# Fourier attention features: query units in pairs of 2048 elements, queries and keys scaled on ScalarE, four slots for the fractions

## The chip, the core and the metric

The kernel runs on one NeuronCore of a Trainium2 chip. PE is TensorE, ACT ScalarE, DVE VectorE, POOL GpSimd and SP SyncE; each runs its own stream of instructions strictly in the order written, and they meet through semaphores. The metric is the device time of one execution in microseconds (us). The kernel before was run three times: median 1554.88 us, from 1553.38 to 1557.7.

## The reference

The program is a two-layer decoder over 64 sequences of 64 tokens with 128 features (4096 tokens): self-attention, cross-attention, an expert layer, then a self-attention with Fourier features, a latent cross-attention and a quantised feed-forward layer. The change lies in the fourth step alone:

```python
def _fourier_kernel(x, proj_mat):
    p = jnp.einsum('blhd,dm->blhm', x, proj_mat) / math.sqrt(D_HEAD)
    return jnp.concatenate([jnp.cos(p), jnp.sin(p)], axis=-1) / math.sqrt(D_KMAP)
q = (x @ Wq.T + bq).reshape(Bv, Lv, N_HEAD, D_HEAD)
k = (x @ Wk.T + bk).reshape(Bv, Lv, N_HEAD, D_HEAD)
v = (x @ Wv.T + bv).reshape(Bv, Lv, N_HEAD, D_HEAD)
q_prime = _fourier_kernel(q, proj_mat)
k_prime = _fourier_kernel(k, proj_mat)
kv = jnp.einsum('blhm,blhd->bhmd', k_prime, v)
out = jnp.einsum('blhm,bhmd->blhd', q_prime, kv)
return out.reshape(Bv, Lv, D_MODEL) @ Wo.T + bo
```

There are 16 heads of 8 features, and 128 projections for each head, so every token has 2048 angles for its keys and 2048 for its queries; each needs a sine and a cosine.

## The kernel before

The Fourier stage works in 8 groups g of 512 tokens (four tiles of 128). A group has 16 units, numbered n; N counts them through all groups. A unit is 128 x 1024 angles: units 0 to 7 are the key half (two units for each tile of tokens, tokens on the partitions), units 8 to 15 the query half (two heads each, projections on the partitions, 512 tokens). The angles are held in turns, not radians.

The path of a unit:
- PE, `angles`: four matmuls into a pair of PSUM banks; there are two such pairs, so the angles of unit N wait until unit N - 2 is reduced. L895 for keys, L897 for queries.
- DVE, `reduce_`: `whole` is the angle rounded by adding and subtracting a large constant (L1258), `frac` the angle less that (L1266). For units 2, 5, 7, 10, 12 and 14 (`ON_SCALAR`) the first addition is made by ACT (`lift`, L1090, into `lifted`) and DVE does one instruction (L1263). Then `wrap` is the absolute value of `frac` (L1268). frac and wrap have three slots; a slot is free when the features of the unit three before are made.
- ACT, `features`: a sine of `frac` (L1082); behind it, where unit N + 2 is one of `ON_SCALAR`, the lift of that unit; then a cosine, which is a sine of a quarter turn less `wrap` (L1086). The results go to `feats` (keys) or `qf` (queries).
- PE, key half: `key_values` (L916) accumulates features times values; ACT copies the sum (`keep_kv`, L1096), PE turns it (L948), ACT copies it (`keep_turned`, L1114). There are two such halves for a group.
- PE, query half: for every two units `outputs` (L961), which ACT copies (`keep_o`, L1102); in the next group, behind its angles 4, `combine` (L975) multiplies with the output weights, and DVE adds the result to the stream (`residual`).
- Between these, the next group is prepared: PE transposes its tokens (L860), ACT copies them (`columns_of`, L1062), PE multiplies for keys (L867) and values (L869), DVE scales and shifts the keys (`keys`, L1234) and the values (L1242), then PE multiplies for the queries (L874) and DVE scales them (`queries`, L1249).

The order is written out by hand: each engine has one loop over N, and the conditions on n in it say what stands behind which unit. At n = 10 PE does the angles of unit 12, the outputs of units 8 and 9, and the transposes of the next group's tokens; the angles of unit 13 follow only then. The outputs wait for the cosine of unit 9 and for the second `keep_turned`.

Of the kernel before, what the change touches and what calls it, by code (L numbers as in the profile page):

```python
# [17 lines left out]
I32 = mybir.dt.int32  # L18
ALU = mybir.AluOpType
# [3 lines left out]
P = 128  # L23
# [686 lines left out]
def experts_and_fourier_phase(nc, ctx, c, name):  # L710
# [15 lines left out]
    KEYS = T * KU  # L726
    UPG = KEYS + Q4 * 2
    ALL = G * UPG
    RING = 3
    MAGIC = 1.5 * 2.0 ** 23  # L730
    TWO_PI, HALF_PI = 6.2831850, 1.5707962
    xs, xT = sb("xs", [P, T, P]), sb("xT", [P, T * P])
# [1 line left out]
    qT, kT = sb("qT", [P, T * P]), sb("kT", [P, T * P])  # L734
    projX = sb("projX", [P, H, M])
    vS = sb("vS", [P, 2, T // 2, H, 32])
    lifted = sb("lifted", [P, 2, UNIT])
    whole, frac, wrap = sb("whole", [P, UNIT]), sb("frac", [P, RING, UNIT]), sb("wrap", [P, RING, UNIT])
    feats = sb("feats", [P, RING, 8, 2, M])
    qf = sb("qf", [P, 2, 4, 2, T * P])  # L740
    kvs = sb("kvs", [P, Q4, 2, M])
# [51 lines left out]
    with nc.Block() as block:  # L793
# [237 lines left out]
        def _(act):  # L1031
# [32 lines left out]
            def features(N):  # L1064
                g, n = divmod(N, UPG)
                act.wait_ge(s["reduced"], N + 1)
                if n < KEYS:
                    used = g * KEYS + n - RING + 1 if n >= RING else g * KEYS
                    if used >= 1:
                        act.wait_ge(s["kv_ps"], used)  # L1070
                    sin, cos = feats[:, n % RING, :, 1, :], feats[:, n % RING, :, 0, :]
                    view = lambda a: a.rearrange("p (h m) -> p h m", m=M)
                else:
                    v = n - KEYS
                    if v % 2 == 0:
                        used = g * Q4 + v // 2 - 1
                        if used >= 1:
                            act.wait_ge(s["o_ps"], used)
                    h = (v % 2) * 2
                    sin, cos = qf[:, (v // 2) % 2, h:h + 2, 1, :], qf[:, (v // 2) % 2, h:h + 2, 0, :]  # L1080
                    view = lambda a: a.rearrange("p (h m) -> p h m", h=2)
                nc.scalar.activation(sin, view(frac[:, N % RING, :]), ACT.Sin, scale=-TWO_PI if n in ON_SCALAR else TWO_PI)  # L1082
                if N + 2 < ALL and (n + 2) % UPG in ON_SCALAR:
                    lift(N + 2)
                act.wait_ge(s["wrapped"], N + 1)
                nc.scalar.activation(cos, view(wrap[:, N % RING, :]), ACT.Sin, bias=half_pi[:, :], scale=-TWO_PI).then_inc(s["feats"], 1)  # L1086

            def lift(N):
                act.wait_ge(s["z_ps"], N + 1)
                nc.scalar.activation(lifted[:, lifts_before(N) % 2, :], angles_at(N), ACT.Copy, bias=MAGIC).then_inc(s["lifted"], 1)  # L1090

            def keep_kv(g, pair):
                act.wait_ge(s["kv_ps"], g * KEYS + 4 * pair + 4)
# [38 lines left out]
            for N in range(ALL + 5):  # L1132
                g, n = divmod(N, UPG)
                if g < G:
# [3 lines left out]
                        act.wait_ge(e["measured"], 2 * G)  # L1138
                    if N == KEYS - 2:
                        root(3, LATE)  # L1140
                    features(N)
                    if 3 <= N <= 6:
                        keep_products(N - 3)
                    if n == 4:
                        keep_kv(g, 0)
                    if g == 0 and n == 8:
# [8 lines left out]
                        keep_o(g, (n - KEYS - 3) // 2)  # L1155
                    if n == 10 and g + 1 < G:
                        columns_of(g + 1)
                if g == G and n == 0:
                    act.wait_ge(s["var"], 1)
                    nc.scalar.activation(c["rstd"][:, 0:MEASURED], c["rstd"][:, 0:MEASURED], ACT.Sqrt)  # L1160
                    nc.scalar.activation(rstdc[:, :], rstdc[:, :], ACT.Sqrt).then_inc(s["root"], 1)
# [8 lines left out]
        def _(dve):  # L1170
# [80 lines left out]
            def reduce_(N):  # L1251
                n = N % UPG
                z = angles_at(N)
                if n in ON_SCALAR:
                    dve.wait_ge(s["lifted"], lifts_before(N) + 1)
                else:
                    dve.wait_ge(s["z_ps"], N + 1)
                    nc.vector.tensor_scalar(whole[:, :], z, MAGIC, MAGIC, ALU.add, ALU.subtract).then_inc(s["rounded"], 1)  # L1258
                    dve.wait_ge(s["rounded"], N - lifts_before(N) + 1)
                if N >= RING:  # L1260
                    dve.wait_ge(s["feats"], N - RING + 1)
                if n in ON_SCALAR:
                    nc.vector.scalar_tensor_tensor(frac[:, N % RING, :], lifted[:, lifts_before(N) % 2, :], MAGIC, z,  # L1263
                                                   ALU.subtract, ALU.subtract).then_inc(s["reduced"], 1)
                else:
                    nc.vector.tensor_tensor(frac[:, N % RING, :], z, whole[:, :], ALU.subtract).then_inc(s["reduced"], 1)  # L1266
                dve.wait_ge(s["reduced"], N + 1)
                nc.vector.tensor_scalar(wrap[:, N % RING, :].bitcast(I32), frac[:, N % RING, :].bitcast(I32), 0x7FFFFFFF, None,  # L1268
                                        ALU.bitwise_and).then_inc(s["wrapped"], 1)

            def residual(g):
                x = c["stream"][:, g * T:(g + 1) * T, :]
# [81 lines left out]
            for N in range(ALL + 6):  # L1354
# [12 lines left out]
                if g < G:  # L1367
                    reduce_(N)
                    if g + 1 < G:
                        if n == KEYS + 5:  # L1370
                            keys(g + 1)
                            values(g + 1)
                if 1 <= g < G and n == 2:
                    queries(g)
                if g >= 1 and n == 4:
                    residual(g - 1)

# [1142 lines left out]
```

## Time and profile before

| what | value |
|---|---|
| median of three runs | 1554.88 us |
| profiled execution, its own time | 1560.69 us |
| its span, first to last instruction | 1558.9 us |
| PE busy over the span | 1414.6 us, 91% |
| DVE busy | 1120.7 us, 72% |
| ACT busy | 972.1 us, 62% |
| POOL busy | 297.5 us, 19% |
| mean granted TensorE clock | 0.976 |

The page cuts the span into 40 slices and gives each engine's busy share in tenths, one digit a slice. The Fourier stage lies in slices 14 to 23, where DVE shows mostly nines and ACT eights and nines:

```profile
PE   6999999998899788888988878999999999999984
PEld 4666666666566344343443355666666666666653
DVE  4666778886434899999999953455667776776788
ACT  2333367676554988998889943445655565665546
```

The shares over the whole span are means over six steps with different limits; what the changed step is limited by has to be read inside it.

### The profile page before, as it was taken

The numbers are of one execution on the slowest core, as the hardware profiler recorded it, in microseconds if no ns is written. First come the engines' busy times: TensorE is split into PE (matmuls) and PEld (weight loads), VectorE is DVE, ScalarE is ACT, GpSimd is POOL, SyncE is SP. The second block draws the span as 40 slices with busy tenths as digits, with TensorE's granted clock in tenths as the row PEclk, the third lists the DMA queues.
The fourth block names the chain that finished last, engine by engine and source line by source line (L and its number), as shares of the span: only waits on it lengthen the run. The fifth ranks groups of instructions, "written<-read, shape, count | busy, mean of one in ns | idle before, by whom it ended". The sixth has DMA issues, their size and how long they took to land. (4 is left out here: it accounts for less than half of the span.)

```text
span 1558.9 us, 32291 instructions
## 1 busy us (share of the span) xinstructions
PE 1414.6 (91%) x12651; PEld 869.2 (56%) x12666; DVE 1120.7 (72%) x2362; ACT 972.1 (62%) x1510; POOL 297.5 (19%) x274
## 2 busy tenths in 40 slices
PE   6999999998899788888988878999999999999984
PEld 4666666666566344343443355666666666666653
DVE  4666778886434899999999953455667776776788
ACT  2333367676554988998889943445655565665546
POOL 3433244452001011110110031111111112220000
PEclk9999999999899999999999989999999999999996
DMA  5000000000100000000000002222222222222210
GB/s 184 2 2 2 2 15 16 13 9 3 55 1 1 1 1 1 1 2 1 1 1 4 1 15 54 61 65 65 65 58 70 63 61 62 62 58 61 69 45 21
DMA packets 40246, 49.74 MB, mean 32 GB/s; under 512 B 8992, under 2 KB 22944, under 8 KB 39712
## 3 DMA queue, kind: packets, MB, share of 16 engines
q1 hardware_dynamic: 39808, 47.01, 11.8%
q8 instruction: 102, 1.67, 0.5%
q10 hardware_dynamic: 288, 0.67, 0.1%
q14 instruction: 48, 0.39, 0.1%
HBM read 13.04 MB, written 2.10 MB: 10 GB/s over the span
## 5 line engine op out<-in xcount | busy, mean ns | idle before, releaser
L2055 DVE TENSOR_TENSOR l_px<-psum,l_share 128x1024 f32<-128x1024 f32 x64 | 78.3, 1224 | 152.7 <-PE psum L1562 103.2
L1800 ACT ACTIVATE l_prob<-psum,l_bias 128x1024 f32<-128x1024 f32 x64 | 71.3, 1114 | 174.7 <-PE psum L1533 174.7
L1545 PE MATMUL psum<-l_XT,l_A 128*128 128x256 f32 x512 | 127.3, 394 | 1.5 <-ACT l_XT L1818 1.5
L1528 PE MATMUL psum<-l_th,l_XT 128*128 128x512 f32 x256 | 125.5, 613 | 1.4 <-DVE stream L2062 0.7
L1562 PE MATMUL psum<-l_prob,l_X 128*128 128x512 f32 x256 | 121.4, 596 | 0.7 <-DVE l_px L2055 0.7
L1608 PE MATMUL psum<-l_px,l_N 128*128 128x256 f32 x480 | 115.0, 383 | 0.0
L2032 DVE TENSOR_REDUCE l_top<-psum 128x8 bf16<-128x1024 f32 x64 | 78.1, 1220 | 36.5 <-PE psum L1625 36.5
L1545 PEld LDWEIGHTS psum<-l_XT,l_A 128*128 128x128 f32 x512 | 94.7, 195 | 12.7 <-ACT l_XT L1818 1.7
L1266 DVE TENSOR_TENSOR f_frac<-psum,f_whole 128x1024 f32<-128x1024 f32 x80 | 97.9, 1224 | 2.7
L1258 DVE TENSOR_SCALAR f_whole<-psum 128x1024 f32<-128x1024 f32 x80 | 97.3, 1217 | 1.6 <-PE psum L895 1.6
L1608 PEld LDWEIGHTS psum<-l_px,l_N 128*128 128x128 f32 x480 | 87.6, 190 | 16.1 <-issue 5.0
L1805 ACT COPY l_th<-psum 128x1024 f32<-128x1024 f32 x64 | 64.8, 1012 | 47.5 <-PE psum L1545 47.5
L408 ACT ACTIVATE a_probT<-psum 128x1024 f32<-128x1024 f32 x32 | 32.7, 1023 | 98.6 <-PE psum L199 98.6
L895 PE MATMUL psum<-f_projX,f_kT 64*128 64x512 f32 x256 | 74.0, 654 | 21.4 <-DVE f_frac L1266 10.6
L1268 DVE TENSOR_SCALAR f_wrap<-f_frac 128x1024 int32<-128x1024 int32 x128 | 88.8, 694 | 4.4
L669 POOL TENSOR_TENSOR a_KX<-a_KT,const 128x1024 f32<-128x1024 f32 x32 | 60.8, 1902 | 115.1 <-ACT a_KT L375 91.0
L480 DVE TENSOR_TENSOR a_prob<-psum,relbias 128x1024 f32<-128x1024 f32 x32 | 39.2, 1224 | 58.0 <-PE psum L185 52.5
L897 PE MATMUL psum<-f_qT,f_projX 64*128 64x512 f32 x256 | 72.1, 639 | 9.6 <-DVE f_frac L1266 9.5
L399 ACT ACTIVATE c_QX<-c_QT,const 128x128 f32<-128x128 f32 x256 | 78.5, 403 | 0.0
L916 PE MATMUL psum<-f_feats,f_vS 128*32 128x256 f32 x1024 | 69.4, 389 | 7.7 <-ACT f_feats L1086 3.7
L1082 ACT ACTIVATE f_feats<-f_frac 128x1024 f32<-128x1024 f32 x64 | 67.6, 1056 | 12.9 <-DVE f_frac L1266 12.9
L2355 POOL TENSOR_TENSOR l_hn<-l_hh,late_weights 128x1024 f32<-128x1024 f32 x12 | 28.2, 2349 | 246.6 <-DVE l_hh L2113 246.6
(353 smaller groups left out, 3193.4 us busy)
## 6 DMA issues: line engine op xcount, KB each, us to landing
l_share<-l_recip SPq DMA_DIRECT2D x496, 64.0 KB, 2.0
early_weights<-in_weights SPq DMA_DIRECT2D x1, 2405.0 KB, 11.4
c_cs<-in_ctx SPq DMA_DIRECT2D x16, 128.0 KB, 2.1
f_qf<-in_l_mats SPq DMA_DIRECT2D x1, 2048.0 KB, 7.7
out<-l_normed SPq DMA_DIRECT2D x16, 128.0 KB, 2.0
l_craw<-in_ctx SPq DMA_DIRECT2D x15, 128.0 KB, 2.3
late_weights<-in_weights SPq DMA_DIRECT2D x1, 1089.0 KB, 11.2
relbias<-in_relbias ACTq DMA_DIRECT2D x1, 512.0 KB, 5.2
```

What stands on the lines that cost most here:

```text
L399: last = nc.scalar.activation(QX[:, n % 3, :, j, :], QT[:, d % DUOS, t * P:(t + 1) * P].rearrange("p (b s) -> p b s", s=S), ACT.Copy, scal ...
L895: last = nc.tensor.matmul(out, kT[rows, t * P:(t + 1) * P], projX[rows, h:h + 4, :], start=True, stop=True)
L897: last = nc.tensor.matmul(out, projX[rows, n - KEYS + 8 * q, :], qT[rows, :], start=True, stop=True)
L1258: nc.vector.tensor_scalar(whole[:, :], z, MAGIC, MAGIC, ALU.add, ALU.subtract).then_inc(s["rounded"], 1)
L1266: nc.vector.tensor_tensor(frac[:, N % RING, :], z, whole[:, :], ALU.subtract).then_inc(s["reduced"], 1)
L1268: nc.vector.tensor_scalar(wrap[:, N % RING, :].bitcast(I32), frac[:, N % RING, :].bitcast(I32), 0x7FFFFFFF, None, ALU.bitwise_and).then_in ...
L1528: nc.tensor.matmul(ps[:, SC + n, :], XT[:, q % 3, k, :, :], th[:, q % 2, k, 8 * n:8 * n + 8, :], start=True, stop=False)
L1545: last = nc.tensor.matmul(ps[:, at + j // 2, (j % 2) * 256:(j % 2 + 1) * 256], A[:, QB * k + j, :], XT[:, q % 3, :, 1, :], start=True, sto ...
L1562: last = nc.tensor.matmul(ps[:, at + n, :], X[:, q % 2, k, :], prob[:, b % 4, n, :], start=True, stop=True)
L1608: last = nc.tensor.matmul(ps[:, YB, 0:256], N[:, h, :], px[:, q % 2, h, :, :], start=(h == 0), stop=(h == H - 1))
L2032: nc.vector.tensor_reduce(top[:, b % 4, :], ps[:, RO:RO + 2, :].rearrange("p a (j n) -> p (a j) n", n=P), AX.X, ALU.max, negate=True).then ...
L2055: nc.vector.tensor_tensor(px[:, q % 2, :, k, :], ps[:, at:at + 2, :].rearrange("p a (h s) -> p (a h) s", s=S), share[:, (b // 2) % 2, b % ...
```

## The change

The units of the query half are made into features two at a time. DVE still reduces each unit by itself, but takes the absolute value of both fractions of a pair in one instruction of 2048 elements behind the second; ACT does one sine and one cosine over 2048 elements for a pair. The lifts of units 10, 12 and 14 move on ACT: 10 stands alone at n = 8, 12 and 14 stand behind the pair (8, 9) and the pair (10, 11). `frac` and `wrap` have four slots in place of three. ACT writes its lift into the frac slot itself, in place of the tile `lifted`, and waits for that slot to be free. The sign of `frac` is now the same in all units. Scaling the queries and the keys of groups 1 to 7 moves from DVE to ACT; those of group 0 stay on DVE.

```diff
-    RING = 3
+    RING, FRACS = 3, 4
...
-    lifted = sb("lifted", [P, 2, UNIT])
-    whole, frac, wrap = sb("whole", [P, UNIT]), sb("frac", [P, RING, UNIT]), sb("wrap", [P, RING, UNIT])
+    whole, frac, wrap = sb("whole", [P, UNIT]), sb("frac", [P, FRACS, UNIT]), sb("wrap", [P, FRACS, UNIT])
...
+            def query_features(N):
+                g, n = divmod(N, UPG)
+                v = n - KEYS
+                at = N % FRACS
+                act.wait_ge(s["reduced"], N + 2)
+                used = g * Q4 + v // 2 - 1
+                if used >= 1:
+                    act.wait_ge(s["o_ps"], used)
+                sin, cos = qf[:, (v // 2) % 2, :, 1, :], qf[:, (v // 2) % 2, :, 0, :]
+                view = lambda a: a[:, at:at + 2, :].rearrange("p n (h m) -> p (n h) m", h=2)
+                nc.scalar.activation(sin, view(frac), ACT.Sin, scale=-TWO_PI)
+                act.wait_ge(s["wrapped"], N + 2)
+                nc.scalar.activation(cos, view(wrap), ACT.Sin, bias=half_pi[:, :], scale=-TWO_PI).then_inc(s["feats"], 2)
+                if n + 4 in ON_SCALAR:
+                    lift(N + 4)
...
             def lift(N):
                 act.wait_ge(s["z_ps"], N + 1)
-                nc.scalar.activation(lifted[:, lifts_before(N) % 2, :], angles_at(N), ACT.Copy, bias=MAGIC).then_inc(s["lifted"], 1)
+                if N >= FRACS:
+                    act.wait_ge(s["feats"], N - FRACS + 1)
+                nc.scalar.activation(frac[:, N % FRACS, :], angles_at(N), ACT.Copy, bias=MAGIC).then_inc(s["lifted"], 1)
+
+            def queries(g):
+                act.wait_ge(s["q_ps"], g + 1)
+                nc.scalar.activation(qT[:, :], ps[:, k_bank(g), :], ACT.Identity, bias=qb[:, :], scale=turn_scale).then_inc(s["q_sb"], 1)
+
+            def keys(g):
...
-                    features(N)
+                    if n < KEYS:
+                        features(N)
+                    elif n % 2 == 1:
+                        query_features(N - 1)
+                    elif n + 2 in ON_SCALAR and n == KEYS:
+                        lift(N + 2)
                     if 3 <= N <= 6:
                         keep_products(N - 3)
+                    if g >= 1 and n == 2:
+                        queries(g)
...
+                    if n == 12 and g + 1 < G:
+                        keys(g + 1)
...
+                units = 2 if n >= KEYS else 1
                 dve.wait_ge(s["reduced"], N + 1)
+                if units == 2 and n % 2 == 0:
+                    return
+                at = (N + 1 - units) % FRACS
+                if N >= FRACS:
+                    dve.wait_ge(s["feats"], N - FRACS + 1)
+                nc.vector.tensor_scalar(wrap[:, at:at + units, :].bitcast(I32), frac[:, at:at + units, :].bitcast(I32), 0x7FFFFFFF, None,
+                                        ALU.bitwise_and).then_inc(s["wrapped"], units)
...
                         if n == KEYS + 5:
-                            keys(g + 1)
                             values(g + 1)
-                if 1 <= g < G and n == 2:
-                    queries(g)
```

The order on ACT in the query half, from the first `keep_turned` (L1114, later L1130) of a group that has a next group. f_frac -> f_qf is a query sine, f_wrap -> f_qf a cosine, f_lifted or f_frac from psum a lift, f_kvs `keep_kv`, f_xT the copy of the next tokens. Before:

```order
L1114 COPY f_kvm<-psum 128x1024
L1082 ACTIVATE f_qf<-f_frac 128x2x512
L1090 ACTIVATE f_lifted<-psum 128x1024
L1086 ACTIVATE f_qf<-f_wrap,f_half_pi 128x2x512
L1096 COPY f_kvs<-psum 128x1024
L1082 ACTIVATE f_qf<-f_frac 128x2x512
L1086 ACTIVATE f_qf<-f_wrap,f_half_pi 128x2x512
L1114 COPY f_kvm<-psum 128x1024
L1082 ACTIVATE f_qf<-f_frac 128x2x512
L1090 ACTIVATE f_lifted<-psum 128x1024
L1086 ACTIVATE f_qf<-f_wrap,f_half_pi 128x2x512
L1062 COPY f_xT<-psum 128x512
```

After:

```order
L1130 COPY f_kvm<-psum 128x1024
L1098 ACTIVATE f_frac<-psum 128x1024
L1112 COPY f_kvs<-psum 128x1024
L1088 ACTIVATE f_qf<-f_frac 128x4x512
L1090 ACTIVATE f_qf<-f_wrap,f_half_pi 128x4x512
L1098 ACTIVATE f_frac<-psum 128x1024
L1130 COPY f_kvm<-psum 128x1024
L1061 COPY f_xT<-psum 128x512
L1088 ACTIVATE f_qf<-f_frac 128x4x512
L1090 ACTIVATE f_qf<-f_wrap,f_half_pi 128x4x512
L1098 ACTIVATE f_frac<-psum 128x1024
L1118 COPY f_oT<-psum 128x512
```

Between the first `keep_turned` and the copy of f_xT stand units 8, 9 and 10 with their lifts of 10 and 12 before, and only units 8 and 9 with the same two lifts after; unit 10 is now part of a double sine and cosine behind the copy.

The order on DVE in the same half, from the reduction of unit 12 (its lifted form, f_frac from a lifted angle) through that of unit 15; f_whole and f_frac reduce, f_wrap is the absolute value, f_kT the keys, f_vS the values. Before:

```order
L1263 SCALAR_TENSOR_TENSOR f_frac<-f_lifted,psum 128x1024
L1268 TENSOR_SCALAR f_wrap<-f_frac 128x1024
L1258 TENSOR_SCALAR f_whole<-psum 128x1024
L1266 TENSOR_TENSOR f_frac<-psum,f_whole 128x1024
L1268 TENSOR_SCALAR f_wrap<-f_frac 128x1024
L1234 TENSOR_SCALAR f_kT<-psum,f_kb 128x512
L1242 SCALAR_TENSOR_TENSOR f_vS<-psum,f_vb 64x32x8 x4
L1263 SCALAR_TENSOR_TENSOR f_frac<-f_lifted,psum 128x1024
L1268 TENSOR_SCALAR f_wrap<-f_frac 128x1024
L1258 TENSOR_SCALAR f_whole<-psum 128x1024
L1266 TENSOR_TENSOR f_frac<-psum,f_whole 128x1024
L1268 TENSOR_SCALAR f_wrap<-f_frac 128x1024
```

After:

```order
L1282 SCALAR_TENSOR_TENSOR f_frac<-f_frac,psum 128x1024
L1285 TENSOR_SCALAR f_whole<-psum 128x1024
L1289 TENSOR_TENSOR f_frac<-f_whole,psum 128x1024
L1297 TENSOR_SCALAR f_wrap<-f_frac 128x2048
L1267 SCALAR_TENSOR_TENSOR f_vS<-psum,f_vb 64x32x8 x4
L1282 SCALAR_TENSOR_TENSOR f_frac<-f_frac,psum 128x1024
L1285 TENSOR_SCALAR f_whole<-psum 128x1024
L1289 TENSOR_TENSOR f_frac<-f_whole,psum 128x1024
L1297 TENSOR_SCALAR f_wrap<-f_frac 128x2048
```

Four absolute values of 1024 became two of 2048, each behind the second unit of its pair, and the keys are gone from before the values.

## Rows read from the trace of the kernel before

**Rows 1.** Busy times by window, of one group's period; first the view's columns.

```profile
core 0: us, PE busy (x) PEld busy (x) DVE busy (x) ACT busy (x) POOL busy (x), PEclk, DMA share, GB/s
...
560.54:608.83 48.29, 42.46 (x418) 19.41 (x416) 46.37 (x59) 43.89 (x48) 5.28 (x5) 1.00 0.01 2
```

**Rows 2.** Groups of instructions of DVE, 505 to 900 us: the absolute value.

```profile
L1268 DVE TENSOR_SCALAR f_wrap<-f_frac 128x1024 int32<-128x1024 int32 x128 | 88.8, 694 | 4.4
```

**Rows 3.** Timeline of group 1, query half: start, duration, engine, line, operation.

```profile
587.11 1.13 PE L897 MATMUL psum<-f_qT,f_projX 64*128 64x512 f32 x4
...
588.17 1.07 PE L916 MATMUL psum<-f_feats,f_vS 128*32 128x256 f32 x16
...
590.63 1.02 ACT L1096 COPY f_kvs<-psum 128x1024 f32<-128x1024 f32 x1
591.52 1.08 ACT L1082 ACTIVATE f_qf<-f_frac 128x1024 f32<-128x1024 f32 x1
...
592.48 1.16 ACT L1086 ACTIVATE f_qf<-f_wrap,f_half_pi 128x1024 f32<-128x1024 f32 x1
...
593.52 1.02 ACT L1114 COPY f_kvm<-psum 128x1024 f32<-128x1024 f32 x1
...
594.68 1.93 PE L961 MATMUL psum<-f_qf,f_kvm 128*32 128x256 f32 x32 [0.83 <-ACT f_kvm L1114]
...
595.37 1.04 ACT L1090 ACTIVATE f_lifted<-psum 128x1024 f32<-128x1024 f32 x1
...
596.44 1.22 DVE L1263 SCALAR_TENSOR_TENSOR f_frac<-f_lifted,psum 128x1024 f32<-128x1024 f32 x1 [0.89 <-ACT f_lifted L1090]
...
597.13 1.13 PE L897 MATMUL psum<-f_qT,f_projX 64*128 64x512 f32 x4
597.31 0.61 ACT L1062 COPY f_xT<-psum 128x512 f32<-128x512 f32 x1
...
598.31 1.22 DVE L1258 TENSOR_SCALAR f_whole<-psum 128x1024 f32<-128x1024 f32 x1
...
601.44 0.75 DVE L1234 TENSOR_SCALAR f_kT<-psum,f_kb 128x512 f32<-128x512 f32 x1
602.10 1.72 DVE L1242 SCALAR_TENSOR_TENSOR f_vS<-psum,f_vb 64x256 f32<-64x256 f32 x4
...
608.83 1.22 DVE L1258 TENSOR_SCALAR f_whole<-psum 128x1024 f32<-128x1024 f32 x1
```

**Rows 4.** Timeline: the key half of group 1, and one row of group 2.

```profile
568.63 0.75 DVE L1249 TENSOR_SCALAR f_qT<-psum,f_qb 128x512 f32<-128x512 f32 x1
...
570.30 3.71 PE L975 MATMUL psum<-early_weights,f_oT 128*64 128x128 f32 x64
...
575.12 1.03 ACT L1090 ACTIVATE f_lifted<-psum 128x1024 f32<-128x1024 f32 x1 [2.27 <-PE psum L895]
...
614.47 1.13 PE L895 MATMUL psum<-f_projX,f_kT 64*128 64x512 f32 x4
```

**Rows 5.** Groups of instructions of ACT, 505 to 900 us: cosine, sine, lift.

```profile
L1086 ACT ACTIVATE f_qf<-f_wrap,f_half_pi 128x1024 f32<-128x1024 f32 x64 | 74.0, 1156 | 0.0
...
L1082 ACT ACTIVATE f_qf<-f_frac 128x1024 f32<-128x1024 f32 x64 | 69.0, 1078 | 2.7 <-DVE f_frac L1266 2.7
...
L1090 ACT ACTIVATE f_lifted<-psum 128x1024 f32<-128x1024 f32 x48 | 49.3, 1026 | 18.8 <-PE psum L895 17.9
```

**Rows 6.** Groups of instructions of ACT, whole span: shorter forms.

```profile
L1054 ACT ACTIVATE f_qf<-f_qf 128x512 f32<-128x512 f32 x32 | 20.2, 630 | 1.0
...
L1844 ACT ACTIVATE l_r<-psum,l_deq 128x512 f32<-128x512 f32 x26 | 16.2, 672 | 0.5 <-DMA c_cs<-in_ctx 0.5
```

**Rows 7.** Timeline of group 0, query half.

```profile
539.70 1.09 PE L948 MATMUL psum<-const,f_kvs 128*128 128x128 f32 x8
...
545.22 1.03 ACT L1114 COPY f_kvm<-psum 128x1024 f32<-128x1024 f32 x1
```

**Rows 8.** Timeline of the last group: the last cosine.

```profile
897.83 1.18 ACT L1086 ACTIVATE f_qf<-f_wrap,f_half_pi 128x1024 f32<-128x1024 f32 x1
```

More of the change, by code:

```diff
@@ L1072, in features @@
                     view = lambda a: a.rearrange("p (h m) -> p h m", m=M)
[L1073 to L1082, printed above, removed]
+                nc.scalar.activation(sin, view(frac[:, N % FRACS, :]), ACT.Sin, scale=-TWO_PI)
                 if N + 2 < ALL and (n + 2) % UPG in ON_SCALAR:
@@ L1085, in features @@
                 act.wait_ge(s["wrapped"], N + 1)
-                nc.scalar.activation(cos, view(wrap[:, N % RING, :]), ACT.Sin, bias=half_pi[:, :], scale=-TWO_PI).then_inc(s["feats"], 1)
+                nc.scalar.activation(cos, view(wrap[:, N % FRACS, :]), ACT.Sin, bias=half_pi[:, :], scale=-TWO_PI).then_inc(s["feats"], 1)
+            def query_features(N):
[13 more added lines that the diff above has]
+                    lift(N + 4)
             def lift(N):
                 act.wait_ge(s["z_ps"], N + 1)
-                nc.scalar.activation(lifted[:, lifts_before(N) % 2, :], angles_at(N), ACT.Copy, bias=MAGIC).then_inc(s["lifted"], 1)
+                if N >= FRACS:
[5 more added lines that the diff above has]
+            def keys(g):
+                act.wait_ge(s["k_ps"], g + 1)
+                nc.scalar.activation(kT[:, :], ps[:, k_bank(g), :], ACT.Identity, bias=kb[:, :], scale=turn_scale).then_inc(s["k_sb"], 1)
             def keep_kv(g, pair):
@@ L1253, in reduce_ @@
                 z = angles_at(N)
+                part = frac[:, N % FRACS, :]
                 if n in ON_SCALAR:
                     dve.wait_ge(s["lifted"], lifts_before(N) + 1)
+                    nc.vector.scalar_tensor_tensor(part, part, MAGIC, z, ALU.subtract, ALU.subtract).then_inc(s["reduced"], 1)
                 else:
@@ L1259, in reduce_ @@
                     dve.wait_ge(s["rounded"], N - lifts_before(N) + 1)
[L1260 to L1266, printed above, removed]
-                dve.wait_ge(s["reduced"], N + 1)
-                nc.vector.tensor_scalar(wrap[:, N % RING, :].bitcast(I32), frac[:, N % RING, :].bitcast(I32), 0x7FFFFFFF, None,
-                                        ALU.bitwise_and).then_inc(s["wrapped"], 1)
+                    if N >= FRACS:
+                        dve.wait_ge(s["feats"], N - FRACS + 1)
+                    nc.vector.tensor_tensor(part, whole[:, :], z, ALU.subtract).then_inc(s["reduced"], 1)
+                units = 2 if n >= KEYS else 1
+                dve.wait_ge(s["reduced"], N + 1)
+                if units == 2 and n % 2 == 0:
+                    return
+                at = (N + 1 - units) % FRACS
+                if N >= FRACS:
+                    dve.wait_ge(s["feats"], N - FRACS + 1)
+                nc.vector.tensor_scalar(wrap[:, at:at + units, :].bitcast(I32), frac[:, at:at + units, :].bitcast(I32), 0x7FFFFFFF, None,
+                                        ALU.bitwise_and).then_inc(s["wrapped"], units)
             def residual(g):
```

## The prediction

> **What bounds the kernel now.** I first read the busy times by window, to see how full the engines are where the change works. Eight groups of 16 units run from 504 to 897 us. Six of them, from group 1 on, have the same period of 48.29 us, in which DVE is busy 46.37 us, ACT 43.89 and PE 42.46, at a granted TensorE clock of 1.00 [rows 1]. So the first suspicion is DVE at 96%, and the absolute values are 128 instructions of 694 ns there [rows 2]. The timeline must say whether DVE is truly never kept waiting. In the query half of group 1 it waits once, 0.89 us, for the lift of unit 12, and its next unit (13, at 598.31) starts the moment that the angles of unit 13 end on PE (597.13 + 1.13 = 598.26) [rows 3]. These angles stand on PE behind a chain through ACT: keep_kv 590.63, keep_turned 593.52, outputs 594.68, transposes of the next tokens, angles 13. ACT works without a gap from keep_kv to its copy of xT at 597.31. Two engines are thus equally late at that place: DVE has about a microsecond to spare there, and ACT's order of work sets when PE may go on. In the key half PE's combine (3.71 us from 570.30) holds back the angles of unit 5, for which ACT waits 2.27 us before its lift at 575.12 [rows 4].
>
> **The change part by part.** Start-to-start times decide on a full queue. For ACT I read them in rows 3: sine to cosine 0.96, cosine to the next 1.04 (its 1.16 less an overlap of 0.12), a 1024 copy 0.89; and for a lift 0.91 (its 1.03 less the same overlap).
>
> *One sine and one cosine over 2048.* The trace has no such instruction. From below: a 1078 ns sine [rows 5] against a 630 ns SBUF form of 512 elements [rows 6] gives 448 ns for 512, or 0.83 to 0.90 for 1024 more; from above: 1.08 and 1.16, as if nothing were saved. I take 0.85, so a double sine occupies ACT 1.81 us and a double cosine 1.89. A pair costs 3.70 in place of 4.00 in four instructions, 1.2 us less of ACT per group. The Trainium skill ("ScalarE: Activation LUTs", What ACT_TABLE_LOAD costs) gives 186 ns + 0.833 ns an element, 280 with a bias pointer, and 93 ns of overlap. The single forms in rows 5 agree within 4%, and by it the double forms would occupy 1.80 and 1.89.
>
> *One absolute value over 2048.* Bounds: the cost of one, 0.69, and of two, 1.39. A single one holds DVE 0.61, since the next starts at the overlap of 0.08; I take 1.15 for the double, between 0.7 and 1.22. That is 0.3 us less of DVE per group (four pairs of 1.22 against 1.15), between nothing and 2.1.
>
> *Keys and queries on ACT.* DVE loses 0.66 twice (601.44 to 602.10 in rows 3; the same form at 568.63 in rows 4). ACT gains two scaled copies of 512 from PSUM with a pointer, whose like takes 672 ns [rows 6], 0.57 start to start. Below, a plain 512 copy's 0.46; above, 0.67. Behind the queries at n = 2 stand sine 3 and the lift of unit 5, which waits 2.27 us for PE: hidden. Behind the keys stand the sine and cosine of units 12 and 13.
>
> *Four slots.* DVE's only wait in rows 3 is the lift's, none is for a slot, so the fourth slot gives nothing but the room that pairs need. The lift into the frac slot adds a wait: the lift of unit 12 now stands behind ACT's own double cosine and waits until it has ended, 0.12 + 0.04 us.
>
> *The order on ACT.* This is what costs. Before, ACT reaches keep_turned at 593.52 after sine 8, lift 10, cosine 8, keep_kv, sine 9, cosine 9. And between keep_turned and the copy of xT it has three instructions of unit 10 to do while PE works. Now, on ACT: keep_turned, lift 10, keep_kv, double sine, double cosine, lift 12, keep_turned, copy of xT, all ahead of the next double sine. Laid out for group 1 from the rows:
> - angles 10 on PE end at 588.24 and key_values 7 at 588.17 + 1.07 = 589.24, as before. The key features ahead of them don't change. The lift of unit 10 starts at 588.28, keep_kv at 589.28.
> - Double sine 590.17, double cosine 591.98; its end, 593.98, releases the lift of unit 12 at 594.02.
> - keep_turned 594.93, in place of 593.52: 1.41 later. Outputs, transposes, angles 13, xT and DVE's unit 13 all follow it with the distances of rows 3: outputs 596.09, angles 13 at 598.54, xT at 598.72, DVE's unit 13 at 599.72 in place of 598.31. ACT meanwhile stands idle from 595.82 to 598.72. DVE would be ready for unit 13 at 598.31 - 0.89 (the lift is there in time now) - 0.75 (two double absolute values in place of five single ones) = 596.67, and waits 3.05 us for PE.
> - From 598.31 to the next group's first unit at 608.83 DVE takes 10.52 us. It loses 0.66 for the keys. It does two double absolute values where three single ones stood (two of 1.15 for three of 0.61): +0.47. That is 10.33; the next group starts at 610.05, 1.22 late. I looked at what could be later still: the lift of unit 14 (after the double cosine that starts at 601.00) ends at 604.06, wanted by DVE at about 605.1; the angles of unit 15, behind the outputs that wait for the same cosine, end at 606.12, wanted at 606.36. Both fit.
> - The last double cosine of the group ends at 612.95. Behind it PE does outputs and then angles 3 of the next group, at 615.83, where 614.47 [rows 4] plus 1.22 would be 615.69: 0.14 more. From there key_values, combine, angles 5 and lift 5 follow back to back on PE and ACT as in rows 4. The 0.66 of the queries that DVE no longer has ends at this gate: DVE only meets the lift of unit 7 a few tenths early, and what it gains by that ACT can't use, for it works from lift 5 through cosine 7 without a gap.
>
> So a full group costs 1.22 + 0.14 = 1.36 us more, and there are six: 8.2. In group 0 the turn of the first key-value half on PE (539.70 + 1.09) gates keep_turned at 540.83; keep_kv 541.72, double sine 542.61, double cosine 544.42, lift 12 546.46, keep_turned 547.37 against 545.22 [rows 7]: +2.15, less 0.19, plus 0.14 = 2.1. The last group has no next tokens, but its last features come in one piece: the same layout from its rows ends the last cosine at 900.12 in place of 897.83 + 1.18 = 899.01 [rows 8]: 1.1. Sum: 8.2 + 2.1 + 1.1 = 11.4 us. Against the profiled execution's own 1560.69 us that is 1572.1; the median of the three runs is 1554.88, to which I add the same: 1566.3.
>
> The Trainium skill ("VectorE: DVE Perf Modes", The TRN2 errata) says that a fixed latency is paid between instructions, so that large tiles pay it once, and that one should tile larger. That rule speaks for this change; what it would yield is the first rival.
>
> **Rivals.**
> *DVE bounds and the waits move.* If ACT's order had slack at the copy of xT, each full group would win on DVE the keys and queries 1.32, the absolute values 0.28 and the 0.89 wait: 2.5 us. Six groups 15, less in the first and last: about 14 us, 1541. The 96% of rows 1 speak for it. Against it: the distance from keep_turned to DVE's unit 13 in rows 3 is all PE and ACT, with no gap that could absorb 1.4 us. It decides if PE could do angles 13 before the transposes, which its order forbids.
>
> *Partly given back.* If DVE's 0.66 at the queries did carry through the key half, a full group would cost 1.36 - 0.66 = 0.7, and all 4.2 + 3.2 = 7.4: 1562. If the double forms also lay at 0.83 and the double absolute value near 0.7, a pair would be 0.04 shorter and the tail after unit 13 0.9 shorter: 0.7 - 0.9 - 0.1 = -0.3 a group, -1.8 for six, against 3.2 for the first and last: 1.4 in all, 1556.
>
> *Double forms that save nothing.* At 1.08 and 1.16 more, keep_turned comes 0.54 later, and the second pair's end another 0.54 later, which then passes the 0.24 of room at unit 15: 0.8 to 1.1 a group, 7 to 9 us more: 1574.
>
> **How the numbers follow.** Forecast 65%, its own range 1562 to 1570; double forms that save nothing 8%; partly given back 14%, of which half lies within 0.3%; DVE bounds 10%; 3% for what I don't see. The range from 1551 to 1574 reaches over the second and third rival and leaves out DVE's. 0.3% (4.7 us) is about what a measurement of this kernel tells from no change. Faster 0.11, same 0.09, slower 0.80.
>
> **What would show it.** In the changed profile: a period of 49.6 us for groups 1 to 6; an idle time of ACT of about 2.9 us before each copy of xT in them, ended by PE's transposes; DVE waiting about 3 us for the angles before unit 13, and no longer for the lift of unit 12; the double sine near 1.93 and the double cosine near 2.01 us; ACT's wait before lift 5 shorter than 2.27 but there. DVE's busy time falls by about 1.3 per group although the time rises. I am wrong if the period is below 48.3 or if ACT's idle time before xT is under 1 us.

## The result, and the profile after

The changed kernel takes 1586.24 us (median of five runs, 1583.97 to 1587.9), the kernel before 1553.38 in its five (1551.07 to 1557.7): a ratio of 1.0199, 95% interval 1.018 to 1.0219. It is slower, as forecast, but by 2.0% and not by the 0.7% that I forecast: 1566.3 was 20 us too low, and 1586 lies outside my range, which ended at 1574.

The profiled execution took 1587.9 us with a span of 1586.1. A group now takes 52.0 to 52.7 us (from one residual's statistics on DVE to the next, mean 52.39 over five groups; the sixth takes 51.2) against 48.29 [rows 1], where I forecast 49.65. The stage, from DVE's first rounding to the aggregation of the last residual's statistics, takes 433.45 us in place of 405.87: 27.6 more, about the difference of the profiled spans, 27.2. The medians differ by 32.9, 5.3 more than the stage: the profiled execution of the kernel before took 1560.69 us, 7 above its median, that of the changed kernel only 2 above. The work ahead of the stage ends anywhere between 499 and 506 us in the profiles below, so I leave these few microseconds open and compare the stage.

The timeline of the changed kernel, query half of group 1, corresponds to rows 3. L1098 is the lift, L1112 `keep_kv`, L1088 and L1090 the double sine and cosine, L1130 `keep_turned`, L960 the outputs, L859 the transposes, L1061 the copy of xT, L1285 DVE's rounding (of unit 13 at 605.28, of the next group's unit 0 at 616.03), L1297 the absolute value:

```profile
591.10 1.02 ACT L1098 ACTIVATE f_frac<-psum 128x1024 f32<-128x1024 f32 x1 [0.44 <-PE psum L896]
...
592.12 1.01 ACT L1112 COPY f_kvs<-psum 128x1024 f32<-128x1024 f32 x1
...
593.03 1.92 ACT L1088 ACTIVATE f_qf<-f_frac 128x2048 f32<-128x2048 f32 x1
...
594.21 1.13 PE L896 MATMUL psum<-f_qT,f_projX 64*128 64x512 f32 x4
594.85 1.99 ACT L1090 ACTIVATE f_qf<-f_wrap,f_half_pi 128x2048 f32<-128x2048 f32 x1
...
596.93 1.02 ACT L1098 ACTIVATE f_frac<-psum 128x1024 f32<-128x1024 f32 x1
597.85 1.00 ACT L1130 COPY f_kvm<-psum 128x1024 f32<-128x1024 f32 x1
...
599.00 3.64 PE L960 MATMUL psum<-f_qf,f_kvm 128*32 128x256 f32 x32 [3.66 <-ACT f_kvm L1130]
...
602.57 1.12 PE L859 MATMUL psum<-const,f_xs 128*128 128x128 f32 x4
...
603.73 0.59 ACT L1061 COPY f_xT<-psum 128x512 f32<-128x512 f32 x1 [4.87 <-PE psum L859]
...
605.28 1.23 DVE L1285 TENSOR_SCALAR f_whole<-psum 128x1024 f32<-128x1024 f32 x1 [6.07 <-PE psum L896]
...
607.85 1.53 DVE L1297 TENSOR_SCALAR f_wrap<-f_frac 128x2048 int32<-128x2048 int32 x1
...
616.03 1.22 DVE L1285 TENSOR_SCALAR f_whole<-psum 128x1024 f32<-128x1024 f32 x1
```

Up to `keep_turned` it is the layout to 0.1 us: from the lift of unit 10 to it 6.75, laid out as 6.65. What isn't in the layout is the next row. PE is idle for 3.66 us before the outputs, and the outputs then take 3.64 where they took 1.93, the transposes 1.12 where they took 0.66. From `keep_turned` to DVE's unit 13 it is 7.43 us; in rows 3 it was 4.79. The windows of the same kernel give the clock of just this stretch, as PEclk:

```profile
core 0: us, PE busy (x) PEld busy (x) DVE busy (x) ACT busy (x) POOL busy (x), PEclk, DMA share, GB/s
...
599.00:605.28 6.28, 6.28 (x41) 2.97 (x42) 0.21 (x1) 1.55 (x2) 1.48 (x2) 0.56 0.01 3
```

Granted is 0.56 of full speed, nearly all of it at the lower of TensorE's two levels, 1.2 GHz in place of 2.4. The outputs take 1.71 us more than before, the transposes 0.46, the angles of unit 13 0.41 (1.54 for 1.13): 2.58 of the 2.64 that are added between `keep_turned` and unit 13. The waits of PE show the gap in all eight groups, and the outputs behind it take 2.92 to 3.64 us in all eight:

```profile
PE psum L960 <- ACT f_kvm L1130: 29.3, 8, 3.7
```

The double forms cost what was worked out (estimates were 1.93 and 2.01 us). The groups of instructions of ACT, then of DVE:

```profile
L1090 ACT ACTIVATE f_qf<-f_wrap,f_half_pi 128x2048 f32<-128x2048 f32 x32 | 63.9, 1996 | 0.0
L1088 ACT ACTIVATE f_qf<-f_frac 128x2048 f32<-128x2048 f32 x32 | 61.3, 1917 | 3.4 <-DVE f_frac L1289 3.4
```

```profile
L1297 DVE TENSOR_SCALAR f_wrap<-f_frac 128x2048 int32<-128x2048 int32 x32 | 42.5, 1329 | 2.9
```

The double absolute value is 1.23 us where nothing disturbs it and up to 1.96 where POOL works at the same time, 1.33 in the mean.

### The profile page after: what moved, and what is told of

Read it like the earlier page. It is cut to its first block and busy times, and to the rows that moved or that the text cites. A ratio compares the mean times of both kernels' runs of the same rounds, so it can differ in the third digit from the quotient of the medians.

```text
span 1586.1 us, 32364 instructions
## 1 busy us (share of the span) xinstructions
PE 1427.5 (90%) x12666; PEld 873.5 (55%) x12666; DVE 1114.2 (70%) x2316; ACT 973.6 (61%) x1460; POOL 292.4 (18%) x274
## 5 line engine op out<-in xcount | busy, mean ns | idle before, releaser
L1285 DVE TENSOR_SCALAR f_whole<-psum 128x1024 f32<-128x1024 f32 x80 | 97.6, 1220 | 45.1 <-PE psum L896 42.5
L960 PE MATMUL psum<-f_qf,f_kvm 128*32 128x256 f32 x1024 | 75.6, 445 | 40.1 <-ACT f_kvm L1130 29.3
L1289 DVE TENSOR_TENSOR f_frac<-f_whole,psum 128x1024 f32<-128x1024 f32 x80 | 97.7, 1221 | 2.7
L1297 DVE TENSOR_SCALAR f_wrap<-f_frac 128x1024 int32<-128x1024 int32 (+1 forms) x96 | 86.9, 905 | 5.1
L960 PEld LDWEIGHTS psum<-f_qf,f_kvm 128*32 128x32 f32 x1024 | 35.8, 124 | 87.2 <-issue 51.4
L1417 POOL TENSOR_SCALAR f_xs<-stream,moments,rstd 128x128 f32<-128x128 f32 x28 | 21.9, 796 | 293.0 <-PE psum L859 292.8
```

What stands on the lines that cost most here:

```text
L960: last = nc.tensor.matmul(ps[32 * r:32 * r + 32, 4 + q % 2, toks], kvm[:, pair, q, e, 32 * r:32 * r + 32], qf[:, q % 2, r, e, toks], start ...
L1289: nc.vector.tensor_tensor(part, whole[:, :], z, ALU.subtract).then_inc(s["reduced"], 1)
L1297: nc.vector.tensor_scalar(wrap[:, at:at + units, :].bitcast(I32), frac[:, at:at + units, :].bitcast(I32), 0x7FFFFFFF, None, ALU.bitwise_an ...
```

## The experiments

Every kernel is compared with the kernel before on the same chip; ratios have 95% intervals. "Period" is the distance of the residuals' statistics on DVE between full groups; "stage" is as in the section above, from each run's profile.

| run | median us | ratio to before | period us | stage us |
|---|---|---|---|---|
| before | 1553.38 | 1 | 48.3 | 405.9 |
| after | 1586.24 | 1.0199 (1.018 to 1.0219) | 52.0 to 52.7 | 433.5 |
| e1_fill | 1577.49 | 1.0128 (1.0098 to 1.0159) | 50.5, then 51.1 | 423.4 |
| e2_kq_back | 1584.52 | 1.0168 (1.0135 to 1.02) | 51.2 | 428.3 |
| e3_kq_only | 1552.53 | 0.9968 (0.9951 to 0.9985) | 47.65 | 398.4 |
| e4_turned_early | 1548.74 | 0.9955 (0.9937 to 0.9972) | 47.2 to 48.3 | 402.3 |
| e5_lift_early | 1547.65 | 0.9962 (0.9949 to 0.9976) | 47.4 | 399.4 |
| e6_delay_only | 1591.43 | 1.0245 (1.0228 to 1.0262) | 52.2 to 53.8 | 438.0 |
| e7_single_abs | 1573.48 | 1.0132 (1.0115 to 1.015) | 50.3 | 419.5 |
| e8_four_forms | 1592.99 | 1.0254 (1.0239 to 1.0269) | 52.1 to 54.1 | 442.4 |
| e9_single_best | 1545.59 | 0.9933 (0.9912 to 0.9954) | 47.0 | 394.1 |

The kernel before took 1557.63 us in the comparison with e1 to e4, 1554.19 in that with e5 to e8, and 1556.77 in that with e9. So the medians of two rows can differ by a few microseconds for that alone; ratios and stages compare better.

**PE kept busy in the gap.** Only this is added to the changed kernel's PE:

```diff
+                    if n == KEYS + 2:
+                        for _ in range(3):
+                            nc.tensor.matmul(ps[:, 5, :], w("f_wk"), w("f_wo")[:, 0:512], start=True, stop=True)
                     if n >= KEYS + 2 and n % 2 == 0:
                         outputs(g, n // 2 - 5)
```

> The changed kernel with three added matmuls of 128x512 on PE in every group, between the angles of unit 12 and the outputs of units 8 and 9, where PE stands idle for 3.66 us; their result is thrown away. Theory (the idle time costs PE its clock): the outputs fall from 3.1 to 3.6 us back to 1.93, the transposes from 1.12 to 0.66, the granted clock of that stretch from 0.56 to about 1.0; DVE's unit 13 comes 4.8 us behind the start of keep_turned in place of 7.4; 2.6 us less in each of seven groups and about 1.4 in the last: 1566 us (1563 to 1570). Rival (the outputs are slow for what they read or write, the double forms on ACT and DVE): outputs stay above 3 us, and the time at 1586.

More work on PE makes the kernel 9 us faster by the medians and the stage 10 us shorter; 1566 was expected (1563 to 1570), so this is a good part of it and not all. Its timeline in group 1 (L1016 the three added matmuls, which the profile counts as six, L1133 `keep_turned`, L1288 DVE's unit 13, L1424 POOL's addition, L1300 the absolute value):

```profile
592.10 2.84 PE L1016 MATMUL psum<-early_weights 128*128 128x512 f32 x6
...
594.68 1.01 ACT L1133 COPY f_kvm<-psum 128x1024 f32<-128x1024 f32 x1
...
595.83 1.93 PE L960 MATMUL psum<-f_qf,f_kvm 128*32 128x256 f32 x32 [0.89 <-ACT f_kvm L1133]
...
599.53 1.23 DVE L1288 TENSOR_SCALAR f_whole<-psum 128x1024 f32<-128x1024 f32 x1 [3.49 <-PE psum L896]
...
601.67 1.29 POOL L1424 TENSOR_TENSOR stream<-f_xs,early_weights 128x512 f32<-128x512 f32 x1
602.10 1.95 DVE L1300 TENSOR_SCALAR f_wrap<-f_frac 128x2048 int32<-128x2048 int32 x1
```

`keep_turned` to unit 13 is 4.85 in all seven groups with a next one, close to the 4.79 of rows 3, and the outputs behind the gap take 1.93; the granted clock from 595.83 to 599.50 is 1.00. So the clock is the cause of that part. What is missing: group 1 takes 50.5, later groups 51.1. In groups 2 to 5 the outputs of units 12 and 13 run at the lower level instead (3.3 to 3.6 us). And the absolute value of units 12 and 13 falls under POOL's addition and takes 1.95 in group 1, where it took 1.53 in the changed kernel (in groups 2 and 3 it took 1.94 and 1.96 there too).

**The delay without the pairs.** The kernel before, one copy moved:

```diff
-                    if n == 9:
+                    if n == 10:
                         keep_turned(g, 1)
```

> The kernel before with one thing moved: ACT does the second keep_turned behind the features of unit 10 and not behind those of unit 9. Nothing is paired. Theory (a late keep_turned costs its delay and, by PE's idle time, the clock): keep_turned 2.9 us later, PE idle 3.7 us in place of 0.83, the outputs at 3.1 to 3.6 us and a granted clock near 0.56 behind it, period 53.8, 1594 us (1588 to 1600). Rival (delay alone, the clock in the changed kernel falls for its double forms): period 51.2, outputs 1.93, 1575.

```profile
597.28 1.03 ACT L1114 COPY f_kvm<-psum 128x1024 f32<-128x1024 f32 x1
...
598.46 3.34 PE L961 MATMUL psum<-f_qf,f_kvm 128*32 128x256 f32 x32 [3.73 <-ACT f_kvm L1114]
...
602.42 0.58 ACT L1062 COPY f_xT<-psum 128x512 f32<-128x512 f32 x1 [4.11 <-PE psum L860]
...
705.83 1.94 PE L961 MATMUL psum<-f_qf,f_kvm 128*32 128x256 f32 x32 [3.73 <-ACT f_kvm L1114]
```

This kernel has neither double forms nor a changed engine for anything, and shows the same: 3.73 us of PE idle, outputs of 3.34, 1591 us. So the double size isn't needed for the fall of the clock. The third row, of group 3, shows that the gap doesn't always bring it: behind the same 3.73 us the outputs take 1.94 there and 1.93 in the last group, and 2.44 to 3.34 in the other six. That parts the price. Group 3 takes 52.2 us, 3.9 more than before, without a fall of the clock: most of it is 2.9 for the delay itself and 0.8 because the absolute value of unit 13 now comes behind POOL's addition and takes 1.53 in place of 0.70, which neither theory had. Groups 2 and 4 take 53.8; the 1.6 more are the clock.

**The pair in four instructions.**

```diff
-                nc.scalar.activation(sin, view(frac), ACT.Sin, scale=-TWO_PI)
+                for i in range(2):
+                    nc.scalar.activation(qf[:, (v // 2) % 2, 2 * i:2 * i + 2, 1, :], view(frac, i), ACT.Sin, scale=-TWO_PI)
                 act.wait_ge(s["wrapped"], N + 2)
```

(and the cosine likewise)

> The changed kernel with the pair's sine and cosine in four instructions of 1024 elements in the same place on ACT: sine, sine, cosine, cosine; the features are signalled behind the last. Theory (the place costs, the size gains 0.3 us a pair): keep_turned 0.3 us later, PE idle 3.9 us, 0.3 to 0.9 us a group: 1591 us (1588 to 1594). Rival (the double size itself costs): 1580 or less.

```profile
599.09 3.19 PE L960 MATMUL psum<-f_qf,f_kvm 128*32 128x256 f32 x32 [3.94 <-ACT f_kvm L1132]
```

The total is as expected, and the rival is refuted: with single forms in the same place the kernel is no faster, but 6.8 us slower (1592.99 against 1586.24; the stage 8.9). `keep_turned` comes 8.47 us behind the first one in place of 8.19, and PE's gap is 3.94. The place on ACT is what costs. The 6.8 us are not all saved by the double forms themselves, though. In groups 2, 3 and 5, with periods of 54.0 to 54.1, the outputs of units 12 and 13 run at the lower level as well (3.23 to 3.62 us); in the changed kernel that happens in group 5 alone (3.46). In groups 1 and 4, where it doesn't, the period is 52.1 and 52.2, no longer than the changed kernel's 52.7.

**Single absolute values**, with the three added matmuls kept:

```diff
-                units = 2 if n >= KEYS else 1
+                units = 1
```

> As the run with three added matmuls, but the absolute value over 1024 elements for each unit, behind its own reduction; double sine and cosine kept. Theory (behind unit 13 DVE works without a gap, and a double absolute value there stands for one of two that would have been hidden in the wait, and is held up beside POOL's additions): from unit 13 to the next group 10.0 us in place of 11.2, seven groups: 1569 us (1566 to 1572). Rival (fewer, larger instructions are what saves): 0.3 us a group slower, 1579.

A miss: 1573.5 us, above the 1566 to 1572 expected. The period is 50.28 in each of five groups, and all outputs in them take 1.93; the stage is 3.9 us shorter than with the double values. The ratios of the two runs, 1.0128 and 1.0132, don't tell them apart; only the profiles do, and part of the difference there is the clock. Group 1 compares the two without it, since all its outputs take 1.93 in both: from unit 13 to the next group 10.69 us with single values and 11.17 with double ones, 0.48 less and not the 1.2 of the theory, because even the single value of unit 13 stands under POOL's addition; over the whole group 0.23 less (50.28 against 50.51). So the price of the double value is shown in its place, and it is small; it isn't shown in the total.

```profile
601.37 1.29 POOL L1424 TENSOR_TENSOR stream<-f_xs,early_weights 128x512 f32<-128x512 f32 x1
601.68 1.53 DVE L1300 TENSOR_SCALAR f_wrap<-f_frac 128x1024 int32<-128x1024 int32 x1
```

**Queries and keys back on DVE**

```diff
+                            keys(g + 1)
                             values(g + 1)
+                if 1 <= g < G and n == 2:
+                    queries(g)
```

(and taken out of ACT's loop)

> The changed kernel with the scaling of queries and keys back on DVE, pairs and four slots kept. Theory (the second part of the query half, behind unit 13, runs on DVE without a gap, the key half is gated by PE and ACT): the keys cost 0.66 in each of seven groups, the queries nothing: 1591 us (1589 to 1593). Rival (ACT's load is what the change made too large): ACT wins 1.2 us a group, seven groups: 1578.

A miss: 1584.5, not 1591. The work did cost DVE its 0.66 behind unit 13 (11.80 us from there to the next group, where groups 2 and 3 of the changed kernel take 11.16 and 11.17), but behind this gap the clock didn't fall in the six full groups; the last row is of the last group:

```profile
600.30 1.01 ACT L1130 COPY f_kvm<-psum 128x1024 f32<-128x1024 f32 x1
...
601.46 1.93 PE L960 MATMUL psum<-f_qf,f_kvm 128*32 128x256 f32 x32 [3.31 <-ACT f_kvm L1130]
...
907.81 3.64 PE L960 MATMUL psum<-f_qf,f_kvm 128*32 128x256 f32 x32 [3.32 <-ACT f_kvm L1130]
```

PE's angles of unit 12 wait 0.28 us for DVE here and end 2.15 us ahead of `keep_turned`, not 2.51, so the gap is 3.31 us in place of 3.66. In group 0, which has no queries in its loop, the gap is 3.66 and the outputs take 3.21. But the shorter gap is not the whole reason: in the last group it is 3.32, and the outputs take 3.64.

**Queries and keys alone on ACT**, in the kernel before (the changed kernel's functions, at n = 2 and n = 12).

> The kernel before with only the scaling of queries and keys moved to ACT (queries behind the features of unit 2, keys at n = 12); single features, three slots. Theory: keys win 0.66 in each of seven groups, the queries nothing, since the gate at unit 5 stands on PE: 1549 us (1547 to 1552). Rival (DVE bounds the whole stage): 1.3 a group, 1544. Second rival (ACT is as full as DVE, its cosine of unit 13 comes late): no gain, 1553.

The median, 1552.5 us, is just above the range given; it is 5 us below the kernel before in the same comparison, which is what the theory took off. The period is 48.29 less 0.65: the keys' 0.66 comes through (9.86 us from unit 13 to the next group in place of 10.52), the queries' doesn't (26.3 us from the group's first rounding to the first `keep_turned` in both). DVE gives 0.41 of it back in a longer wait for the lift of unit 12, 1.30 where rows 3 have 0.89:

```profile
590.46 1.22 DVE L1275 SCALAR_TENSOR_TENSOR f_frac<-f_lifted,psum 128x1024 f32<-128x1024 f32 x1 [1.30 <-ACT f_lifted L1090]
```

**Another order for the pairs**

```diff
                 nc.scalar.activation(sin, view(frac), ACT.Sin, scale=-TWO_PI)
+                if n == KEYS:
+                    keep_turned(g, 1)
                 act.wait_ge(s["wrapped"], N + 2)
...
-                    if n == 9:
-                        keep_turned(g, 1)
...
-                    if n >= KEYS + 2 and n % 2 == 0:
+                    if n >= KEYS + 3 and n % 2 == 0:
                         outputs(g, n // 2 - 5)
+                    if n == KEYS + 3:
+                        outputs(g, 0)
```

> The changed kernel with another order at one place: ACT does the second keep_turned between the double sine and the double cosine of units 8 and 9, and PE does the transposes of the next tokens and the angles of unit 13 ahead of the outputs of units 8 and 9. Theory (what costs is that all of ACT's pair stands ahead of keep_turned, and PE idle behind it): PE's idle time before the transposes about 0.6 us, its clock 1.0, DVE's unit 13 about 5.2 us earlier in a group, limited now by the lift of unit 12; period 47.2 in place of 52.4: 1547 us (1543 to 1553), below the kernel before. Rival (pairs of 2048 are late for their users wherever the copies stand): above 1565.

37 us faster than the changed kernel by the medians, and 31 in the stage, with the same instructions; two orders changed, that of one copy on ACT and that of the outputs on PE, and the run doesn't part them. L1134 is `keep_turned`, L859 the transposes, L1284 DVE's unit 12:

```profile
588.62 1.00 ACT L1134 COPY f_kvm<-psum 128x1024 f32<-128x1024 f32 x1
...
589.77 0.63 PE L859 MATMUL psum<-const,f_xs 128*128 128x128 f32 x4 [0.65 <-ACT f_kvm L1134]
...
592.68 1.22 DVE L1284 SCALAR_TENSOR_TENSOR f_frac<-f_frac,psum 128x1024 f32<-128x1024 f32 x1 [0.98 <-ACT f_frac L1102]
```

Groups 3 and 5 are 1 us longer; there the clock falls later, behind two gaps of 0.90 and 0.84 us, which the other groups have too without it:

```profile
697.20 3.62 PE L960 MATMUL psum<-f_qf,f_kvm 128*32 128x256 f32 x32 [0.84 <-ACT f_qf L1094]
```

**The lift ahead of the cosine, and a little work for PE at n = 14** (in the kernel of e4; `filler` is one matmul of 256 columns whose product is overwritten, added to PE on each side of the angles)

```diff
+                    act.wait_ge(s["sined"], g + 1)
+                    lift(N + 4)
...
+                if g < G and n == KEYS + 6:
+                    filler(g)
                 if N + 2 < ALL:
                     angles(N + 2)
+                if g < G and n == KEYS + 6:
+                    filler(g)
```

> As the run with the early keep_turned, and besides: the lift of unit 12 also ahead of the double cosine of units 8 and 9 (it waits for the double sine and the absolute value alone, which are the readers of its slot), and two matmuls of 128x256 on PE at n = 14, around the angles of the next group's unit 0, their result thrown away. Theory: DVE's wait of 0.98 before unit 12 goes, of which 0.6 to 0.9 reaches the next group; the outputs of units 12 and 13, which ran at half the clock (3.6 us) in every second group, take 1.93 in all: period 46.6, stage about 8 us shorter than the kernel before's, 1543 us (1539 to 1548). Rival (ACT, which works without a gap from unit 10's sine into the next group, is the bound now): no faster than the early keep_turned alone, 1549.

The outputs take 1.93 in all full groups and the period is even, 47.4; but what the wait of 0.98 gave is lost again. The absolute value of units 12 and 13 now meets POOL's addition and takes 1.72 us, where it took 1.23 in e4_turned_early, and DVE waits another 0.44 for PE before unit 15:

```profile
592.09 1.29 POOL L1434 TENSOR_TENSOR stream<-f_xs,early_weights 128x512 f32<-128x512 f32 x1
...
592.74 1.72 DVE L1310 TENSOR_SCALAR f_wrap<-f_frac 128x2048 int32<-128x2048 int32 x1
```

The total, 1547.65, lies inside the range of the theory and at the value of the rival, and its interval overlaps that of e4_turned_early. No gain is shown over it; that ACT is the bound is not shown either.

**The better version, without pairs**

```diff
+                if n + 2 == KEYS + 4:
+                    lift(N + 2)
                 nc.scalar.activation(sin, view(frac[:, N % RING, :]), ACT.Sin, scale=-TWO_PI if n in ON_SCALAR else TWO_PI)
```

(with e3_kq_only's move and PE's order as in e4_turned_early)

> The kernel before with queries and keys scaled on ACT, single features and three slots, and two changes of order: ACT lifts unit 12 ahead of the sine of unit 10, and PE does the transposes and the angles of unit 13 ahead of the outputs of units 8 and 9. Theory: DVE's wait of 1.30 us before unit 12, which keys and queries on ACT alone leave, falls to about 0.3, nothing else comes late: period 46.8 in place of 47.65, 1543 us (1540 to 1548), faster than all before it. Rival (PE's keys and values, which still follow the outputs, or ACT, which has hardly a gap left, hold the group at the old pace): 47.6, 1549.

```profile
588.58 0.63 PE L860 MATMUL psum<-const,f_xs 128*128 128x128 f32 x4 [0.83 <-ACT f_kvm L1126]
...
589.40 1.22 DVE L1279 SCALAR_TENSOR_TENSOR f_frac<-f_lifted,psum 128x1024 f32<-128x1024 f32 x1 [0.36 <-ACT f_lifted L1094]
```

0.9933 of the kernel before, 11 us, and 2.6% below the changed kernel by the ratio of the ratios. PE's gap is 0.83, DVE's wait before unit 12 0.36 in place of 1.30. It is the fastest in these runs; its interval still overlaps those of e4 and e5.

## Why the prediction was right in direction and wrong in size

The later `keep_turned` came as predicted and set the direction; what it did to PE was missing from the sum. For the first full group (group 1, 52.67 us, 4.38 more than before), and for the six from group 1 on together:

| step | forecast, group 1 | measured, group 1 | forecast, six | measured, six |
|---|---|---|---|---|
| `keep_turned` later | 1.41 | 1.51 | 8.5 | 9.0 |
| `keep_turned` to DVE's unit 13 | 0 | 2.64 | 0 | 11.7 |
| unit 13 to the next group | -0.19 | +0.23 | -1.1 | +2.1 |
| next group's start to its first `keep_turned` (angles 3 late) | 0.14 | 0 | 0.8 | 0.6 |
| sum | 1.36 | 4.38 | 8.2 | 23.4 |

Group 1 is one of the two dearest: the second step added 2.6 and 2.7 us in groups 1 and 4, and 1.4 to 1.7 in the others, with the clock's fall longer or shorter.

**The step that failed** is "Outputs, transposes, angles 13, xT and DVE's unit 13 all follow it with the distances of rows 3". Those distances were taken at full clock behind a gap of 0.83 us. I had worked out that ACT would stand idle for 2.9 us and DVE for 3.05, but never laid out PE, the engine they both waited for. It had finished the angles of unit 12 at 595.34 and had nothing until 599.00. e1_fill takes the 2.64 away with the gap; in e6_delay_only a later copy alone makes such a loss appear, in six groups of eight. The six periods from group 1 on sum to 313.2 us where they were 289.8: 23.4 more, of which the forecast had 8.2. Of the 15.2 that it lacks, 11.7 lie in this step. The whole stage lacks 27.6 - 11.4 = 16.2.

The trace of before had the price in it. Three rows of its timeline, early key angles of the stage and its last two outputs, none of them among my rows:

```profile
511.80 2.08 PE L895 MATMUL psum<-f_projX,f_kT 64*128 64x512 f32 x4 [3.41 <-DVE f_frac L1266]
...
894.61 1.93 PE L961 MATMUL psum<-f_qf,f_kvm 128*32 128x256 f32 x32 [2.37 <-ACT f_qf L1086]
...
899.06 2.88 PE L961 MATMUL psum<-f_qf,f_kvm 128*32 128x256 f32 x32 [2.51 <-ACT f_qf L1086]
```

2.08 us stands there for what takes 1.13 elsewhere, and 2.88 for 1.93. The row between them kept its 1.93 behind a gap of 2.37 us, so these rows give the price of a fall and a warning, but not when it comes. The Trainium skill ("TensorE: Matmul & The Clock Gate", Why this matters for your kernels) warns of idle gaps between bursts of matmuls for this very reason. In the changed kernel the trace agrees, in all eight groups; in e6_delay_only six of eight do. I weighed two other pages instead of this one.

**The tail behind unit 13** was mis-sized by 0.4 in group 1: a double absolute value of 1.45 start to start for 1.15 beside POOL, and 0.06 more between a fraction and a double value, twice. In groups 2 and 3, where the double value takes 1.94 and 1.96, it was mis-sized by 0.8 (11.16 and 11.17 us in place of 10.33). Working out +0.47 for "two of 1.15 for three of 0.61" was right in sign: one of two values is moved out of a stretch in which DVE waits anyway into one in which it doesn't.

**Right:** the double sine and cosine (1.92 and 2.00 us against 1.93 and 2.01); the lift behind its own cosine; the gap of ACT before xT, 4.87 us, of which 2.9 was forecast and the rest is the clock; that the queries give nothing and the keys 0.66 (e3_kq_only); DVE's wait before unit 13, 6.07 where I had 3.05 plus, again, the clock. The ends: up to the statistics of group 1 the stage took 2.4 us more, where I had 2.1 for group 0, and the last group cost about 1.7 by its interval (44.83 against 43.08), where I had 1.1.

**The rivals:** "DVE bounds" is refuted, DVE's busy time fell (1120.7 to 1114.2 us over the span) and the time rose. "Partly given back" is refuted too: the queries' 0.66 doesn't carry through (e3_kq_only), and the double absolute value takes 1.23 alone, not 0.7. "Double forms that save nothing" is refuted by the rows, 1.92 and 2.00 us for two of 1.08 and 1.16. None of my cases had an upper end above 1574, because all of them kept PE's speed.

What stays open: the 5.3 us between the difference of the medians and that of the stages, and what decides whether the clock falls. It fell behind 3.73 us in six groups of e6_delay_only and not in two, behind gaps of under 1 us in some groups of e4_turned_early and e1_fill and not in others.

## What to carry to other kernels

When a change delays a producer, lay out the idle time of every engine behind it, PE first, and look in the trace for what the same matmuls took behind such a gap: a few microseconds of idle PE were charged twice here, once as the gap and once at half the clock. Fusing two instructions saves their fixed cost (0.3 us a pair here), but everything queued behind them waits for both; put copies that others wait for between the parts. Here the place of one copy on ACT, with PE's order to suit, was worth 31 us of the stage, and fusing sine and cosine 9 at most, part of which was the clock. The best kernel found has no pairs at all.

## What the runs showed of the hardware

- In the changed kernel a gap of 3.66 us of PE was followed by outputs of 2.92 to 3.64 us in place of 1.93 in all eight groups, in group 1 at a granted clock of 0.56. The length of one gap alone doesn't tell, though. Behind 3.73 us in e6_delay_only six groups show 2.44 to 3.34 us and two 1.93 and 1.94; behind 3.31 to 3.35 us in e2_kq_back six groups show 1.93 and the last 3.64; behind two gaps of 0.90 and 0.84 us in a row in e4_turned_early two groups show 3.61 and 3.62 and the others 1.93.
- A DVE absolute value issued at 602.10 while POOL's addition ran from 601.67 to 602.96 (e1_fill) ended at 604.05: 1.95 us in place of 1.23, 1.09 behind POOL's end. The single one at 601.68 in e7_single_abs took 1.53 in place of 0.69. In the kernel before DVE's was issued first and kept its 0.70, and POOL's addition took 1.74 in place of 1.29:

```profile
600.83 0.70 DVE L1268 TENSOR_SCALAR f_wrap<-f_frac 128x1024 int32<-128x1024 int32 x1
600.94 1.74 POOL L1395 TENSOR_TENSOR stream<-f_xs,early_weights 128x512 f32<-128x512 f32 x1
```

  The Trainium skill ("GPSIMD Engine Reference", Specifications) says that GpSimd shares its SBUF interfaces with VectorE, with contention for VectorE instructions in a 2-port perf mode or with two SBUF inputs. The trace agrees that the two hold each other up, and shows that in these rows the one that came first kept its time; in which mode the absolute value ran, no run shows.
